# TensorE reads the upper halves of float32 messages as bfloat16, and the one-hots of an edge block are written node by node

## What is computed

```python
x = x + gnn0(layernorm(x), adj)            # neighbour sum, 128->512, RMS norm, SiLU, 512->128
x = x + ffn0(layernorm(x), edge_index)     # GAT scores over 524288 edges choose 2 of 4 experts
x = x + gnn1(layernorm(x), adj)            # masked softmax attention inside each tile
x = x + ffn1(layernorm(x))                 # router chooses 2 of 8 experts, 128->256->128
```

```python
e     = leaky_relu(a_src[src] + a_dst[dst], 0.2)
alpha = exp(e - max_of(dst)) / (sum_of(dst) + 1e-16)
agg   = segment_sum(h[src] * alpha, dst)   # h has 4 heads of 4 values
```

## Time and profile before

| | us |
|---|---|
| timed, median of 3 | 3447.95 |
| timed, lowest and highest | 3446.22, 3448.56 |
| span of the profiled execution | 3672.8 |
| VectorE busy in it | 2761.0 (75%) |
| TensorE matmul busy | 2583.2 (70%) |
| ScalarE busy | 1723.5 (47%) |
| GpSimd busy | 1169.0 (32%) |

### The profile page before, as it was taken

The page is one execution under the profiler, slowest core; times in us unless marked ns, Lnnn a source line. Parts: engine busy times, 40 slices in busy tenths (PEclk is TensorE's granted clock), DMA queues, the critical chain, the costliest instruction groups (busy, mean ns, idle before and its releaser), DMA issues.

```text
span 3672.8 us, 49655 instructions
## 1 busy us (share of the span) xinstructions
PE 2583.2 (70%) x15405; PEld 1913.6 (52%) x15406; DVE 2761.0 (75%) x8069; ACT 1723.5 (47%) x3052; POOL 1169.0 (32%) x1205
## 2 busy tenths in 40 slices
PE   1888888888888612026777777777777777777889
PEld 0666656656666401014555555555555555555666
DVE  7888778887887546367877777787787787788774
ACT  1566566665665311124454444454444544545544
POOL 0000000000000037655554545555545545555200
PEclk7899999998999855557887877878888788788899
DMA  2111111111110223223223223332232322322200
GB/s 84 34 48 47 44 46 50 44 43 38 50 38 32 72 59 77 49 62 76 63 59 78 61 63 73 66 75 65 58 78 65 73 66 62 75 64 59 76 12 9
DMA packets 228561, 210.53 MB, mean 57 GB/s; under 512 B 70781, under 2 KB 160585, under 8 KB 227657
## 3 DMA queue, kind: packets, MB, share of 16 engines
q1 hardware_dynamic: 190008, 190.83, 17.6%
q0 software_dynamic: 37280, 14.38, 4.5%
q10 hardware_dynamic: 1008, 2.15, 0.2%
HBM read 159.49 MB, written 47.74 MB: 56 GB/s over the span
## 4 chain that ended last, share of the span: by engine, by line
DVE 31%; PE 13%; another core or an unknown queue 8%; issue 8%; POOL 1%; ACT 1%; DVEq 0%; SPq 0%; DMA 0%; POOLq 0%; ACTq 0%
DVE keep_x L2174 7%; PE lay_b_y L1800 6%; PE lay_b_z L1791 5%; DVE lay_oh L1055 2%; POOL lay_got L1754 1%; DVE lay_oht L2079 1%; DVE lay_xn L2209 1%; DVE lay_parts L1068 1%; DVE lay_left L1067 1%; DVE lay_parts L1069 1%; DVE lay_parts L1066 1%; DVE lay_msg L1063 1%; DVE lay_stats L2198 1%; DVE lay_hp L2236 1%
## 5 line engine op out<-in xcount | busy, mean ns | idle before, releaser
L1754 POOL DMA_INDIRECT lay_got<-node_table,lay_idx x1152 | 1145.5, 994 | 928.6 <-PE lay_b_z L1791 326.3
L1800 PEld LDWEIGHTS lay_b_y<-lay_w,lay_hid 128*128 128x128 f32 x4096 | 572.1, 215 | 284.9 <-issue 271.4
L1800 PE MATMUL lay_b_y<-lay_w,lay_hid 128*128 128x128 f32 x4096 | 576.9, 298 | 114.8 <-issue 66.1
L1791 PE MATMUL lay_b_z<-lay_xin,lay_w 128*128 128x512 f32 x1024 | 599.8, 715 | 18.2 <-ACT lay_hid L1945 9.2
L1945 ACT ACTIVATE lay_hid<-lay_b_z,lay_b 128x512 f32<-128x512 f32 x512 | 332.6, 683 | 530.1 <-PE lay_b_z L1791 305.3
L2174 DVE SCALAR_TENSOR_TENSOR keep_x<-lay_b_y,lay_gates,keep_x 128x128 f32<-128x128 f32 x1024 | 287.4, 343 | 273.3 <-remote 175.4
L879 POOL MEMSET find_no_src<- 128x9 int32 x1 | 0.1, 108 | 1252.5 <-POOLq L47 1252.5
L2023 ACT ACTIVATE lay_unused<-lay_hub_wide,lay_halves 128x1152 bf16<-128x1152 uint16 x256 | 320.3, 1251 | 124.5 <-DMA lay_hub_wide<-sorted_dst 100.7
L461 PE MATMUL front_b_h<-front_xt,front_m 128*128 128x512 f32 x512 | 273.6, 666 | 58.8 <-ACT front_act_m L571 30.6
L1791 PEld LDWEIGHTS lay_b_z<-lay_xin,lay_w 128*128 128x128 f32 x1024 | 205.1, 223 | 189.3 <-issue 164.0
L217 DVE TENSOR_TENSOR sort_keys<-sort_keys 128x1024 f32<-128x1024 f32 (+2 forms) x182 | 257.4, 1414 | 37.9 <-ACT sort_keys L539 35.4
(11 more groups left out here) (392 smaller groups left out, 4577.3 us busy)
## 6 DMA issues: line engine op xcount, KB each, us to landing
lay_wide<-sorted_dst SPq DMA_DIRECT2D x128, 288.0 KB
lay_hub_wide<-sorted_dst SPq DMA_DIRECT2D x128, 288.0 KB
made<-front_y SPq DMA_DIRECT2D x128, 256.0 KB, 2.0
lay_y<-made SPq DMA_DIRECT2D x32, 1024.0 KB
lay_got<-node_table,lay_idx POOLq DMA_INDIRECT x1152
front_adj<-in_adj SPq DMA_DIRECT2D x32, 256.0 KB, 3.1
keep_x<-in_x SPq DMA_DIRECT2D x32, 256.0 KB, 3.5
lay_adj<-in_adj SPq DMA_DIRECT2D x32, 256.0 KB
```

What stands on the lines that cost most here:

```text
L1754: pool.indirect_dma_start(out=got[:, b % RING, c, :], out_offset=None, in_=table, in_offset=bass.IndirectOffsetOnAxis(ap=idx[:, b % AHEAD, ...
L1791: pe.matmul(b_z[c][:, :], w1[:, e, P * c:P * c + P], flat(xin[g % 2][:, :, :]), start=True, stop=True).then_inc(z_done, 1)
L1800: mm = pe.matmul(b_y[n % 2][:, P * j:P * j + P], hid[n % 2][:, c, P * j:P * j + P], w2[:, e * HK + c, :], start=(c == 0), stop=(c == HK - 1))
```

## The change

`messages` no longer casts. One float32 buffer `split` [128, 9, 3, 20] takes the place of `msg`, `left` and `parts`; its three rows per column are the message, the message less the upper 16 bits of itself, and that less the upper 16 bits of itself. Each upper half is a bfloat16 number, cut off and not rounded. TensorE and VectorE read these halves in place, as every second bfloat16 element. VectorE's one-hot `oh` becomes [128, 128, 9], columns innermost: a constant `node_col`, in which each node number is repeated 9 times, is compared with the nine numbers of the block, a row of 9 read again for each node. TensorE reads a column of it as weights with elements 9 apart. GpSimd writes `node_col` among the constants. In the loop of `edge_tables` only `messages` changes; its one-hot stays.

```diff
+def high_halves(split):
+    return split.bitcast(BF16).rearrange("p c a (f t) -> p c a f t", t=2)[:, :, :, :, 1]
-def messages(v, me, looked, got, look, msg, left, part):
+def messages(v, me, looked, got, look, split):
+    high = high_halves(split)
+    msg, left, last = (split[:, :, a, :] for a in range(PARTS))
...
-    me.link(v.tensor_copy(part[:, :, 0, :], msg[:, :, :]))
-    me.link(v.tensor_tensor(left[:, :, :], msg[:, :, :], part[:, :, 0, :], ALU.subtract))
-    me.link(v.tensor_copy(part[:, :, 1, :], left[:, :, :]))
-    return v.tensor_tensor(part[:, :, 2, :], left[:, :, :], part[:, :, 1, :], ALU.subtract)
+    me.link(v.tensor_tensor(left, msg, high[:, :, 0, :], ALU.subtract))
+    return v.tensor_tensor(last, left, high[:, :, 1, :], ALU.subtract)
...
-        oh = s.sb("oh", [P, 2, GC, P], BF16)
+        node_col = s.sb("node_col", [P, P, GC], BF16)
+        oh = s.sb("oh", [P, 2, P, GC], BF16)
...
-        msg = s.sb("msg", [P, GC, ROW])
-        left = s.sb("left", [P, GC, ROW])
-        parts = s.sb("parts", [P, 2, GC, PARTS, ROW], BF16)
+        split = s.sb("split", [P, 2, GC, PARTS, ROW])
...
+            pool.iota(node_col[:, :, :], [[1, P], [0, GC]], base=0, channel_multiplier=0,
+                      allow_small_or_imprecise_dtypes=True).then_inc(consts, 1)
...
-                        mm = pe.matmul(b_att[b % 2][:, GC * LOOK:GC * LOOK + SUM], oh[:, b % 2, c, :],
-                                       parts[:, b % 2, c, :, :].rearrange("p a f -> p (a f)"),
+                        mm = pe.matmul(b_att[b % 2][:, GC * LOOK:GC * LOOK + SUM], oh[:, b % 2, :, c],
+                                       high_halves(split[:, b % 2, :, :, :])[:, c, :, :]
+                                       .rearrange("p a f -> p (a f)"),
...
             def hots(b):
-                one_hots(v, oh[:, b % 2, :, :], iota_b, low[:, b, :])
+                v.tensor_tensor(oh[:, b % 2, :, :], node_col[:, :, :], over(low[:, b, :].unsqueeze(1), [P, P, GC]),
+                                ALU.is_equal)
```

More of the change, by code:

```diff
@@ L1125, in edge_tables @@
         look = s.sb("look", [P, GC, HEADS])
-        msg = s.sb("msg", [P, GC, ROW])
-        left = s.sb("left", [P, GC, ROW])
-        parts = s.sb("parts", [P, GC, PARTS, ROW], BF16)
+        split = s.sb("split", [P, GC, PARTS, ROW])
         added = s.sb("added", [P, ROW])
@@ L1281, in _ @@
                 for c in range(GC):
-                    mm = pe.matmul(b_s[:, 0:SUM], oh[:, c, :], parts[:, c, :, :].rearrange("p a f -> p (a f)"),
+                    mm = pe.matmul(b_s[:, 0:SUM], oh[:, c, :], high_halves(split[:, :, :, :])[:, c, :, :]
+                                   .rearrange("p a f -> p (a f)"),
                                    start=(c == 0), stop=(c == GC - 1))
@@ L1418, in _ @@
             with v.Fori(0, n) as g:
-                me.base, me.n = head + 12 * g, 0
+                me.base, me.n = head + 10 * g, 0
                 blk = [v.value_load(block_no[0:1, u, bass.ds(g, 1)], min_val=0, max_val=tiles - 1) for u in range(2)]
@@ L1431, in _ @@
                 v.wait_ge(more_got, (16 * GC) * g + 16 * GC)
-                messages(v, me, b_d[:, 0:GC * LOOK], got[:, :, :], look, msg, left, parts[:, :, :, :])\
+                messages(v, me, b_d[:, 0:GC * LOOK], got[:, :, :], look, split[:, :, :, :])\
                     .then_inc(more_msg, 1)
@@ L1437, in _ @@
                 v.sem_inc(more_free, 1)
-                assert me.n == 12, me.n
+                assert me.n == 10, me.n
 def rank(v, me, T, E, value, mask, beat, tie, out):
@@ L1732, in _ @@
                       allow_small_or_imprecise_dtypes=True).then_inc(consts, 1)
-            pool.wait_ge(consts, 6)
+            pool.wait_ge(consts, 7)
             pool.affine_select(out=ident[:, :], in_=ident[:, :], compare_op=ALU.not_equal, fill=1.0,
@@ L1762, in _ @@
         def _(pe):
-            pe.wait_ge(consts, 9)
+            pe.wait_ge(consts, 10)
             def look_up(b):
@@ L2085, in attend @@
                     v.wait_ge(gathered[b % RING], (16 * GC) * (b // RING + 1))
-                    messages(v, edge, b_att[b % 2][:, 0:GC * LOOK], got[:, b % RING, :, :], look, msg, left,
-                             parts[:, b % 2, :, :, :]).then_inc(msg_ready, 1)
+                    messages(v, edge, b_att[b % 2][:, 0:GC * LOOK], got[:, b % RING, :, :], look,
+                             split[:, b % 2, :, :, :]).then_inc(msg_ready, 1)
                 if has_block(b - 1):
@@ L2273, in choose @@
                                        op0=ALU.is_lt, op1=ALU.mult).then_inc(gates_ready[1], 1)
-            v.wait_ge(consts, 9)
+            v.wait_ge(consts, 10)
             for u in (1, 0):
```

## The result

The changed kernel takes 3388.44 us (3385.49 to 3390.4), against 3447.09 us for the kernel before: the ratio is 0.9826, 95% interval 0.9812 to 0.984. It is 58.7 us faster. The forecast was 3335 us, 112 us faster than that median. The time lies in the stated range of 3295 to 3400 us, but outside rival A's own 3316 to 3370 us, and the gain is about half of the forecast.

A forecast was written before the change was run, and what follows sets the result against it. VectorE was taken as the bound (94% occupied), TensorE close behind. An iteration of 54.9 instead of 58.9 us, 28.25 times, gives 113 us; less 1.1, plus 0.7: 112.6 us off 3447.95, so 3335 us, range 3295 to 3400 us.

The forecast's parts named there:

- rival A: The forecast itself, whole kernel: 3335 us, own range 3316 to 3370 us; chance 0.50.
- C (1352 ns): VectorE's one-hot doesn't speed up and stays at 1352 ns: 3363 us, or 3400 us; chance 0.12.
- D (every second block): Only every second block's one-hot speeds up, odd blocks starting mid-word: 3338 us; chance 0.08.
- Strided loads: TensorE's edge sums: reading one-hot weights 9 elements apart adds up to 0.29 us a block.
- The lists: Each engine's own work per four-block iteration: VectorE 55.3 to 49.9 us, TensorE 49.4 to 50.6 us.
- what is late next: Pipelined iterations: period is the larger list, 50.6 us, plus 4.3 us of waits: 54.9 instead of 58.9 us.
- waits across: VectorE's waits with a nameable releaser, per iteration: 3.6 us before, taken as 4.3 us after, at most twice 3.6.
- unnamed waits: VectorE's idle time without nameable releaser, 1600 to 3450 us: 202.4 us, 7.2 an iteration, taken as the profiler's.
- Rival B: TensorE and ScalarE hold the pace; about half of VectorE's 153 us is lost: 3388 us; chance 0.17.
- E (pairs one by one): TensorE's edge sums can't stream upper halves behind strided weights: 8 us more an iteration, 3507 us; chance 0.05.
- F: All of VectorE's saving counts, and the first 15 blocks' too: 3275 us; chance 0.05.
- Around it: Outside the pipelined iterations: `node_col`'s iota at the start +1.1 us, casts in `edge_tables` -0.75 us, early blocks' saving hidden.

The follow-up runs named there:

- c2: The changed kernel with the old one-hot, so only the casts are gone, against the kernel before: 3393.82 us, ratio 0.9848.
- r3_both: The changed kernel with two moves in VectorE's list (last layer's first expert before the layer norms, logits' shift behind the fourth expert): 3271.63 us, 0.9489 of before.
- r4_both_on_before: The kernel before with two moves in VectorE's list (first expert before the layer norms, shift behind the fourth expert): 3383.32 us, 0.9817 of before.
- s1: The kernel before, with TensorE reading edge-sum weights 9 elements apart (sums wrong): 3684.99 us against 3679.24 us, ratio 1.0003.
- b1_before: The kernel before, unchanged, traced again on a chip of the slower kind: 3686.9 us, beside a median of 3685.48 us there.

## Why the forecast was half right

- **The instructions were right, with two sizes off.** Casts: gone, 0.75 us a block. Subtracts: 345 ns, as taken. One-hot: 818 ns where I took 757, a saving of 0.53 instead of 0.60 us; all blocks alike, so rivals C (1352 ns) and D (every second block) are out. Strided loads: nine sums start over 0.52 to 0.54 us, as taken. The upper halves cost the moving side nothing: with dense weights and upper halves (`c2`) a matmul of the edge sums has a median of 191 ns. The Trainium skill's rule in "Vector Engine (DVE) Microarchitecture Reference", section 5.1 (two results a cycle, and alignment to 4 bytes makes no difference), agrees with 818 ns on blocks with an even and an odd number; the rule of a start aligned to 4 bytes in "Advanced Engine Details and Errata", section "2x-1p Requirements", doesn't: odd blocks start 2 bytes off a 4-byte word and are no slower.
- **The lists were nearly right.** VectorE's was to be 49.9 us; it is 47.8 busy and 3.1 in short gaps, 50.9 us. TensorE's was to be 50.6 us; no row gives that list by itself, its matmuls are busy 47.6 us.
- **The step that failed is "what is late next".** I let the waits across grow from 3.6 to 4.3 us and wrote that they might reach twice 3.6. They are 7.3 us. 50.6 + 4.3 made 54.9 us; 50.9 + 7.3 is 58.2. The difference, 58.16 - 54.9 = 3.26 us, is 92 us over 28.25 iterations. The 4.3 us itself was a guess ("a fifth more"), with no row behind it. I had seen that a saving in the second half only lengthens VectorE's waits, and then summed the two lists as if order did not matter. I didn't follow the one chain that crosses the engines: norms, first expert on VectorE, second product on TensorE, transpose, product, logits, shift on VectorE. In the kernel before, one of its ends was in the rows already: 26.3 us in 21 waits of line 2256 for line 1890. `r3_both` and `r4_both_on_before` show it: with that chain loosened, the waits grow only from 2.7 to 3.8 us (98.2 us over 25.7 iterations), the period is 54.40 us, and the change is worth 111.7 us.
- **The base of the sum was wrong too.** I took the unnamed waits out of a trace of a slower chip and kept the rest: 58.9 us. With the moves, before's period on the chip of 3447 us was 58.37 us. Without the moves it must have been about 58.16 + 61.0 / 28.25 = 60.3 us; this is worked out and not traced. So two errors met: the forecast took a period for before that was 1.4 us too short, and one for after that was 3.3 us too short.
- **Rival B gave 3388 us, and 3388.44 us was measured.** Its core, that about half of VectorE's saving is lost to TensorE's pace, is what happened; but its condition, that the unnamed waits pace the timed run, is not so at 3447 us, and its 16 us for weight loads were at most 8.5 us in `s1`, on the other kind of chip. That its number fits within 1 us is luck. The agreement of 111.7 with 112.6 us is in part luck too: VectorE's list gave 5.1 instead of 5.4 us and its waits grew by 1.2 instead of 0.7 us, and the forecast was meant for the kernel without the moves. E (pairs one by one) didn't occur, and F's early blocks didn't speed up.
- **Around it.** The iota took 2277 ns where I took 1050; still, line 2235 first starts at about 1548 us in the changed kernel and line 2228 at 1547 us in `r4_both_on_before`, so the start hardly moved.

## What to carry to other kernels

When two engines' lists become equally long, the sum of each list no longer gives the period: follow the chains that cross between them, and ask of each instruction that frees a buffer for the other engine what stands in front of it. Here a saving of 5.1 us an iteration brought about 2.2 us (worked out) until one expert of 1 us was moved before the layer norms and the shift behind its neighbour; with both it brought 4.0 us. And where a trace is longer than the timed runs, find out whether it came from another chip before calling the difference the profiler's.

## What the runs showed of the hardware

- One and the same kernel takes about 3447 us on some chips and about 3680 us on others (3679.24 and 3685.48 us). The longer executions have idle time on VectorE with no nameable releaser (161.5 us in 33 waits for experts in `b1_before`), while VectorE's and ScalarE's instructions last as long as elsewhere (an expert's step 342 and 343 ns, GELU 682 and 683 ns, in `b1_before` and `r4_both_on_before`). The slower traces hold a little over half as many semaphore updates (24,665 and 44,541). What causes it was not found.
- A GpSimd iota of 1152 bfloat16 numbers with a repeat of 9 innermost takes 2277 ns, where 128 and 256 numbers in a row take 236 and 338 ns: 2.0 ns an element, not 0.8.
- VectorE's comparison with two 16-bit sources at step 1 takes 818 ns for 1152 elements. If it is two results a tick at the rate of the float32 steps, that leaves 818 - 576 x 1.039 = 220 ns fixed, where the float32 steps have 158 ns.
- bfloat16 numbers at every second element, as the moving side of 60 columns, cost TensorE nothing measurable (medians of 191 and 192 ns).
